# Two layers of cross attention and FFN on one core: the second cross attention unrolled to a slot for each step of a tile

## The reference

```
x += linear_attention(LN(x), ctx)      # 16 heads, gate, Wo                   "stage 0"
x += moe_ffn(LN(x))                    # top 2 of 8 experts + shared expert   "stage 1"
x += norm_delta(softmax_attention(LN(x), ctx, mask))                         # "stage 2"
x += ffn(LN(x) in float16)             # 256 -> 1024 -> 256, exact gelu       "stage 3"

softmax_attention: q = LN(x) Wq + bq; k = ctx Wk + bk; v = ctx Wv + bv   (16 heads of 16)
                   out = softmax(q k / 4, masked) v Wo + bo
norm_delta:        d = rs * out; (d - mean d) / sqrt(var d + 1e-5) * gamma + beta
```

## Time and profile before

| what | value |
|---|---|
| median of 3 runs | 499.48 us (495.07 to 500.86) |
| profiled execution | 501.04 us, span 499.2 us |
| busy, share of the span | PE 424.8 us (85%), DVE 326.5 (65%), POOL 229.5 (46%), ACT 229.2 (46%) |
| mean granted clock of TensorE | 0.896 |
| instructions | 10421 |

### The profile page before, as it was taken

How to read it: one execution, slowest core, us unless ns; L and a number is a source line. 1 busy time by engine, 2 the same in 40 slices (tenths; PEclk the granted TensorE clock), 3 DMA queues, 4 the chain that set the end, 5 groups by cost and what they waited for, 6 DMA issues and landing times. The chain is left out here.

```text
span 499.2 us, 10421 instructions
## 1 busy us (share of the span) xinstructions
PE 424.8 (85%) x3336; PEld 380.8 (76%) x3336; DVE 326.5 (65%) x904; ACT 229.2 (46%) x527; POOL 229.5 (46%) x377
## 2 busy tenths in 40 slices
PE   2999999999879678999985658786988699699995
PEld 1777888888668568999984657675877589699995
DVE  4488778777665855665548565787587747766542
ACT  4476675664332113776765253323242334354450
POOL 4355554885636502123545513777677644721200
PEclk9899998998988979999999697879577958799999
DMA  8622111224102432578653101111101000001011
GB/s 269 188 63 63 46 57 52 84 73 156 44 21 86 169 117 64 178 226 248 194 160 105 44 1 43 33 33 33 33 22 44 21 1 2 1 22 41 25 43 42
DMA packets 31731, 39.30 MB, mean 79 GB/s; under 512 B 4289, under 2 KB 29122, under 8 KB 31682
## 3 DMA queue, kind: packets, MB, share of 16 engines
q1 hardware_dynamic: 28610, 30.29, 19.8%
q0 software_dynamic: 3072, 8.39, 4.9%
HBM read 25.03 MB, written 13.63 MB: 77 GB/s over the span
## 5 line engine op out<-in xcount | busy, mean ns | idle before, releaser
L998 ACT ACTIVATE arena_f<-PS,cols 128x256 f16<-128x256 f32 x64 | 26.6, 471 | 32.4 <-PE PS L2019 30.2
L337 PE MATMUL PS<-wfh,arena_r 128*128 x120 | 36.0, 300 | 3.6 <-DVE arena_f L1445 1.9
L361 POOL TENSOR_TENSOR ve<-mv,eps 128x1 f32<-128x1 f32 x32 | 6.1, 189 | 66.5 <-DVE mv L355 66.4
L337 PE MATMUL PS<-w0h,arena_r 128*128 128x256 f32 (+1 forms) x96 | 36.6, 381 | 0.0
L378 PE MATMUL PS<-ident,arena_f 128*128 128x128 f32 x64 | 15.9, 337 | 23.8 <-DVE arena_f L370 8.5
L720 POOL DMA_INDIRECT raw<-ys_rows,posy x32 | 31.6, 989 | 9.7 <-issue 7.8
L2019 PE MATMUL PS<-arena_r,w1h 128*128 128x256 f32 x128 | 33.4, 298 | 2.0 <-ACT arena_r L1008 1.0
L468 POOL TENSOR_TENSOR w1l<-raw,w1h 128x384 fp32r<-128x384 f32 x16 | 15.0, 935 | 42.4 <-ACT w1h L455 42.4
L338 PE MATMUL PS<-wfl,arena_r 128*128 x120 | 33.9, 283 | 0.0
L339 PE MATMUL PS<-wfh,arena_r 128*128 x120 | 33.6, 280 | 0.0
L2019 PE MATMUL PS<-arena_r,w1l 128*128 128x256 f32 x128 | 32.9, 294 | 0.0
(11 more groups left out here) (278 smaller groups left out, 1524.5 us busy)
## 6 DMA issues: line engine op xcount, KB each, us to landing
arena_f<-xs_rows SPq DMA_DIRECT2D x40, 128.0 KB, 2.3
ys_rows<-raw SPq DMA_DIRECT2D x20, 256.0 KB, 2.5
raw<-in_w_ffn SPq DMA_DIRECT2D x16, 241.0 KB, 2.6
raw<-in_w_l SPq DMA_DIRECT2D x16, 192.0 KB, 3.0
ctx_raw<-in_ctxT SPq DMA_DIRECT2D x16, 128.0 KB
out<-arena_f SPq DMA_DIRECT2D x8, 256.0 KB, 2.1
x<-in_x SPq DMA_DIRECT2D x1, 1792.0 KB, 10.6
raw<-in_w_l SPq DMA_DIRECT2D x2, 512.0 KB, 5.7
```

Of the source, the lines that this page charges most:

```text
L337: nc.tensor.matmul(out_ap, lh, rh, start=first, stop=False)
L998: nc.scalar.activation(md16[:, r, n, :], PS[:, M_H + n // 2, (n % 2) * D:(n % 2 + 1) * D], ACT.Gelu, bias=cols[:, 2 * KC + n:2 * KC + n + ...
```

## The change

It has six parts:

1. The shared expert's outputs use four PSUM banks (`H_O`), so the output of tile t waits for the sum of tile t-3 (earlier: t-1); DVE's order is new, `block_table` stands after the sums of four tiles, and `result_places` in the first expert block.
2. `keys_values(p)` is cut into `keys(p)` and `values(p)`. Those of pairs 0 and 1 are made inside the block loop, and keys of pair 2 before the last down product. Ctx pairs are loaded and split earlier.
3. Gathers have a ring of six tiles; the first nine are issued before the slots.
4. The layer norm before attention and the delta's norm are ACT instructions with scale rstd and bias -mean*rstd. POOL makes both for one x tile and one delta tile, eight tiles apart, in one chain of width two (`joint_rstd`).
5. The bias bo is added on PE, by two matmuls of one row by 256 columns; ACT scales by rs (`delta`); gamma moves from POOL to DVE; POOL adds beta to x early (`add_beta`) and the delta late (`add_delta`).
6. `slot2` has one order for even and odd slots, scores have two banks of their own each (`X_S = (6, 1)`), and the steps of a tile lie more slots apart: 20 slots in place of 19 on DVE, 22 on POOL.

Cut to its core:

```diff
-H_G, H_U, H_O = (3, 6), (5, 1), (4, 2)
+H_G, H_U, H_O = (3, 6), (5, 1), (4, 2, 0, 7)
+LOAD_CTX_AT, CTX_AT, KEYS_AT = (4, 12, 14, 19), (6, 8, 16, 20), (12, 16)
+JOIN = 8
+RING = 6
...
@@ DVE, shared expert @@
+            gate_factor(4)
+            hidden(4)
             for t in range(2):
                 add_shared(t)
-            gate_factor(4)
-            add_shared(2)
-            hidden(4)
-            add_shared(3)
             hidden_lo(4)
+            for t in range(2, 4):
+                add_shared(t)
+            gate_factor(5)
+            hidden(5)
             block_table()
-            result_places()
...
@@ PE, blocks @@
+                if j in KEYS_AT:
+                    keys(KEYS_AT.index(j))
+                if j - 2 in KEYS_AT:
+                    values(KEYS_AT.index(j - 2))
                 if j == BPAIRS + 1:
-                    pe.wait_ge(w_lo, 2 * TILES)
-                    keys_values(0)
+                    keys(2)
...
@@ POOL @@
+            def joint_rstd(n):
+                kinds = slice(0 if n < TILES else 1, 2 if n >= JOIN else 1)
...
+                if n < TILES:
+                    pool.wait_ge(S2["x_moments"], 2 * n + 2)
+                if n >= JOIN:
+                    pool.wait_ge(S2["d_moments"], 2 * (n - JOIN) + 2)
+                nc.gpsimd.tensor_tensor(vej[:, at, kinds], mvj[:, at, kinds, 1], eps[:, 0:wide],
+                                        ALU.add).then_inc(S2["shifted"], 1)
...
+                nc.gpsimd.tensor_tensor(rj[:, at, kinds], vej[:, at, kinds], mhalf[:, 0:wide],
+                                        ALU.pow).then_inc(S2["shifted"], 1)
...
+                for k in range(kinds.start, kinds.stop):
+                    nc.gpsimd.tensor_scalar(sj[:, at, k:k + 1], mvj[:, at, k, 0:1], rj[:, at, k:k + 1], -1.0,
+                                            ALU.mult, ALU.mult).then_inc(S2["shifted"], 1)
...
+            def add_beta(t):
+                pool.wait_ge(xn_ready, LN_BASE[2] + t + 1)
+                nc.gpsimd.tensor_tensor(x[:, t, :], x[:, t, :], rows[:, 3, :], ALU.add).then_inc(S2["beta"], 1)
+            def add_delta(t):
+                pool.wait_ge(S2["beta"], t + 1)
+                pool.wait_ge(S2["scaled"], t + 1)
+                nc.gpsimd.tensor_tensor(x[:, t, :], x[:, t, :], dn[:, t % 2, :], ALU.add).then_inc(x_done[2], 1)
...
             def slot2(s):
+                if s.at + 3 < TILES + JOIN:
+                    joint_rstd(s.at + 3)
...
+                if tile := s.tile(-6):
+                    add_delta(tile[0])
+                if tile := s.tile(9):
                     gather(tile[0])
+                if tile := s.tile(-1):
+                    add_beta(tile[0])
...
@@ ACT @@
+            def norm_x(t):
+                act.wait_ge(S2["shifted"], shift_count(t))
...
+                nc.scalar.activation(xn[:, t % 2, :], x[:, t, :], ACT.Identity, bias=sj[:, t, 0:1],
+                                     scale=rj[:, t, 0:1]).then_inc(xn_ready, 1)
...
             def slot2(s):
+                if tile := s.tile(2):
+                    normed_hi(tile[0])
+                if tile := s.tile(-3):
+                    attended_hi2(tile[0])
+                if tile := s.tile(3):
+                    norm_x(tile[0])
+                if tile := s.tile(0):
+                    probabilities(tile[0])
+                if s.ring == 1 and s.tile(1):
+                    queries((s.at + 1) // 2)
+                if tile := s.tile(-5):
+                    delta_normed(tile[0])
+                if tile := s.tile(-3):
+                    delta(tile[0])
...
@@ PE @@
             def slot2(s):
+                if tile := s.tile(0):
+                    scores(tile[0])
+                if s.ring == 1 and s.tile(1):
+                    pair_queries((s.at + 1) // 2)
+                if tile := s.tile(-1):
+                    weighted_values(tile[0])
+                if s.is_at(TILES + 1):
+                    attended_T2(TILES - 1)
+                if tile := s.tile(-3):
+                    output(tile[0])
+                if (tile := s.tile(-2)) and tile[0] < TILES - 1:
+                    attended_T2(tile[0])
+                if tile := s.tile(3):
+                    normed_T(tile[0])
...
+                if s.is_at(TILES):
+                    pe.wait_ge(S2["clipped"], 2 * TILES)
+                    ffn_hidden(0, 0, EARLY[:4])
+                if s.is_at(TILES + 1):
+                    ffn_hidden(0, 0, EARLY[4:])
```

More of the change, by code:

```diff
@@ L986, in _ @@
+            keys(3)
+            ctx_pair_hi(5)
+            keys(4)
+            norm_x(0)
+            ctx_pair_hi(6)
             keys(5)
+            normed_hi(0)
+            norm_x(1)
             ctx_pair_hi(7)
-            for p in range(6, CPAIRS):
-                keys(p)
-            act.wait_ge(setup_v, 6)
+            keys(6)
+            normed_hi(1)
+            norm_x(2)
+            keys(7)
+            queries(0)
             def ffn_gelu(g, r, features):
@@ L1450, in block_h_lo, with values, heads @@
                                         ALU.subtract).then_inc(E["h_lo"], 1)
+            def values(p):
+                dve.wait_ge(S2["v_psum"], p + 1)
+                dve.wait_ge(S2["zeroed"], 3 * p + 3)
+                def heads(ap, b, h, r):
+                    return ap[SEQ * b:SEQ * (b + 1)].rearrange("p (r g h e) -> p r g h e", r=r, g=PAIRS, h=2)[:, :, :, h, :]
+                for b in range(2):
+                    for h in range(2):
+                        last = nc.vector.tensor_tensor(
+                            vb[p][SEQ * h:SEQ * (h + 1), :, b, :, HD * h:HD * (h + 1)],
+                            heads(PS[:, VALUES_BANK[p], :], b, h, 2),
+                            heads(rows[:, 0, :], b, h, 1).to_broadcast([SEQ, 2, PAIRS, HD]), ALU.add)
+                last.then_inc(S2["vb_ready"], 1)
             for j in range(2):
@@ L1505, in _ @@
             values(2)
             ctx_pair_lo(4)
[L1507 removed]
             values(3)
             ctx_pair_lo(5)
[L1510 removed]
+            entering(0)
             values(4)
             ctx_pair_lo(6)
[L1513 to L1514 removed]
+            entering(1)
+            values(5)
+            normed_lo(0)
+            ctx_pair_lo(7)
             entering(2)
[L1516 to L1517 removed]
@@ L1546, in _ @@
+            normed_lo(1)
+            entering(3)
+            values(7)
             cx = PS[:, X_C, 0:PAIRS * PVC].rearrange("p (g n) -> p g n", g=PAIRS)
@@ L2081, in slot2 @@
-                if s.ring == 0:
-                    if s.tile(0) and not s.is_at(0):
-                        pair_queries(s.at)
-                    if s.tile(-1):
-                        weighted_values(*s.tile(-1))
-                if s.ring == 1 and s.tile(0):
-                    scores(*s.tile(0), s.pair)
-                if s.tile(-2):
-                    output(*s.tile(-2))
-                if tile := s.tile(2):
-                    if before := s.tile(-2):
-                        after(pe, S2["cnT_lo"], before[0])
-                    transpose_x(pe, 2, *tile, X_T)
```

646 lines of the change are left out of this document (344 added, 302 removed).

## The result

Changed kernel: 482.05 us, median of 4 runs (479.88 to 484.76), beside 500.17 us of the kernel before (4 runs, 495.07 to 503.09). Ratio 0.967, 95% interval 0.958 to 0.977. It is faster, by 18 us where the prediction said 38. The profiled execution took 482.49 us (span 480.4, granted clock 0.925); the one of before 501.04.

A forecast was written before the change was run, and what follows sets the result against it. PE was taken to bound expert blocks and FFN, a chain of four engines with PE's falling clock the cross attention. First scores -12, steps -20, end -6 make -38: 501 to 463, said as 462 (454 to 470; 443 to 481 eight in ten).

The forecast's parts named there:

- Shared sums: Shared expert stage: four banks remove PE's waits and slow clock, so the blocks start 8 us earlier (4 to 9).
- Keys in the blocks: Expert blocks: PE's matmuls of two pairs cost 5.8 us, ACT's burst 1, later keys save 1.5: +5.3 us.
- Start: Last block output to first scores: POOL's queue, then ACT, takes 27.9 us instead of 36.8: -9.
- A slot for each step: Cross attention, first to last scores: steps of 5.7, then 6.5 us, plus 8 for the clock, 101 in all: -20.
- the chain through gamma: Late cross attention steps: POOL's delta add waits for DVE's gamma, delaying the next statistics; 6.5 us a step.
- The end: Last scores to steady FFN: 13.5 us instead of 18.49, plus 1 us from the FFN's start: -6 (-9 to -2).
- I take 13.5: Last scores to steady FFN: PE's remaining work 12 us, the last tile's chain 10 plus handoffs; 13.5 us taken.
- a longer queue of POOL and ACT: Cross attention: slower steps or a falling clock, 7.3 to 7.6 us a step, total 474 to 482; chance 0.24.
- The other rivals: Cross attention: no clock drop, 445 us, chance 0.20; steps staying at 8, 487, 0.07; lower clock throughout, 510, 0.04.
- the two drops: Cross attention: two falls of PE's clock, each about 1.3 steps long at 3 us a step, 8 us allowed.
- four fifths: Cross attention: share of steps at the lower clock from which the change would be slower; that rival's chance 0.04.
- The price of nothing: Cross attention: gamma on DVE charged no delay to POOL; the skill's port lock would cost some 4 us, sum 466.
- the bursts to keep the clock falling: Cross attention: short matmul bursts between waits keep lowering PE's clock, sum about 478; chance 0.24, shared with a longer queue.

The follow-up runs named there:

- e10: The kernel before with its shared sums in four banks and DVE's order left alone: 495.60 us, ratio 0.989.
- e13: Changed kernel with half of PE's products for keys and values of pairs 0 and 1 left out: blocks 76.74 us.
- e4: Changed kernel with the keys' evacuation of pairs 0 and 1 ahead of the weight split in ACT's slot: 478.57 us, ratio 0.961.
- e6: Changed kernel with POOL's memsets, gathers and statistics interleaved anew and ACT's contexts of pairs 6 and 7 ahead of norms: 488.89 us, ratio 0.972.
- e11: Changed kernel with the add of delta at the end of POOL's slot: 481.44 us, ratio 0.955.
- e3: Changed kernel with ACT's last attended values around the first four gelus and the second group's halves before the last delta norm: 474.96 us, ratio 0.954.
- e12: Changed kernel with the moves of e3, e4, e5, e6 and e11 together: 463.39 us, ratio 0.923.
- e15: e12 run again unaltered, in another call: 459.90 us, ratio 0.921.
- e8: Changed kernel with the norms of x and of delta on DVE again, slots kept: 499.55 us, ratio 1.002.
- e5: Changed kernel with gathers six tiles ahead in place of nine, one in each slot: 493.29 us, ratio 0.988.

## Why the prediction was wrong, step by step

1. **Shared sums: right in kind, the size in part by luck.** -8 said, -9.6 in the profiles. The banks alone are 5.7 us by e10's ratio; the rest lies within what the shared stage varies by, about 9 us with the same code. The waits are counts: an output of tile t waits until t-3 sums are done, that is for tile t-4 (before: t-1 sums, tile t-2), where the description of the change and the prediction name tile t-3.
2. **Keys in the blocks: wrong in its mechanism.** The step priced PE's matmuls as "5.8 us there in full" and ACT's burst at 1 (0 to 3). Halving the matmuls changed nothing beyond the spread (e13); moving ACT's burst gave 3.8 us back (e4). The 7 us that stay after e4 were not taken apart. I had asked whether ACT has room (45 of 66 us) and not what stands ahead of the keys in its queue and who waits for them.
3. **Start: the size was right for another order.** 27.9 us said, 31.7 measured, 27.7 in e6. The sum let the memsets end about when the store landed, 4.4 us after the last block output; they ended at 6.4. It counted what POOL has to do up to the third statistics and let each item start when POOL was free; ACT and DVE lost time because the statistics of tile 0 stood behind work they did not need.
4. **A slot for each step: right in size, slightly better, partly by luck.** 5.25 us a step from scores 2 to 7 (5.7 said), 6.4 from 8 to 15 (6.5 said); 95.8 us in all against 101. Two errors cancel: the lump of gathers, 8.1 us for the first step, was not seen, and the chain through gamma cost about 7 us once (95.8 us against 89.0 in e11), from slot 6 on, where a gather stands in it, not in every late step: from slot 7 on POOL has no gather left. From scores 9 to 15 a step takes 6.0 us, and 5.9 with the chain undone (e11), so the chain does not set these steps; what does was not tested.
5. **The end: the failed step, 13.9 of the 19 us.** "I take 13.5" summed the chain of the last tile and PE's work of 12 us. ACT's order cost 6.8 us (e3). With that mended PE is busy 15.5 of 19.1 us at the upper clock (e12): its work was 3.5 us more than I counted. A tile now leaves one slot later, so that four outputs and not three are left after the last scores, each with 0.43 us of bias rows, for which step 4 had charged 0.23. The fourth output and these rows are about 2.4 of the 3.5, an estimate from their rows (0.7 us for an output's product and 4 x 0.43). So ACT's order is half of the miss and PE's work a quarter; the last quarter is waits whose causes were not taken apart.

Of the rivals, "a longer queue of POOL and ACT" came nearest: 474 to 482 by a slower step. The time is right, the place is not, the steps were fast. The other rivals did not occur. Two sums of the rivals do not come out, though the forecast does not rest on them: 7.3 to 7.6 us a step are 110 to 114 us, or 118 to 122 with the two drops, not 112 to 118; and (8.05 + 1.2 - 6.3) of 3.2 is nine tenths of the steps, not four fifths.

By the Trainium skill (SBUF — State Buffer, "Who interferes with whom") each gamma on DVE should have held POOL up. The price of nothing was right, but not for the reason given, that such work shows no delay. The timelines of POOL and DVE in the kernel before:

```profile
310.86 0.34 POOL L760 TENSOR_TENSOR ve<-mv,eps 128x1 f32<-128x1 f32 x1 [3.01 <-DVE mv L1536]
311.27 0.82 POOL L763 TENSOR_TENSOR rstd<-ve,mhalf 128x1 f32<-128x1 f32 x1
313.60 0.19 POOL L361 TENSOR_TENSOR ve<-mv,eps 128x1 f32<-128x1 f32 x1 [1.51 <-DVE mv L355]
313.87 0.55 POOL L364 TENSOR_TENSOR rstd<-ve,mhalf 128x1 f32<-128x1 f32 x1
...
318.49 0.73 POOL L755 TENSOR_TENSOR x<-x,arena_f 128x256 f32<-128x256 f32 x1
318.69 0.81 DVE L1467 SCALAR_TENSOR_TENSOR x<-raw,mix,x 128x256 f32<-128x256 f32 x1
...
327.20 0.45 DVE L1467 SCALAR_TENSOR_TENSOR x<-raw,mix,x 128x256 f32<-128x256 f32 x1
```

L1467 and L1471 are DVE's two adds of a combine, with both large operands in SBUF. In nine of 16 tiles they overlap POOL's add L760, and there it takes 0.34 to 0.37 us and the power L763 behind it 0.82; in the other seven 0.19 and 0.55 to 0.56 (in two of these L1467 begins during the power, which stays at 0.56). The other way round, L1467 takes 0.77 to 0.88 us in the five tiles where it starts during POOL's add L755, and 0.45 to 0.51 elsewhere. So in this trace the two engines delay each other, as the Trainium skill has it there; averages such as those in the earlier trace rows hide it. In the changed kernel gamma seldom meets POOL, which mostly stands waiting for it: of nine gammas in the stage one overlaps a POOL instruction, a shift that took 0.47 us and not 0.26. At the end, where they meet again, both get longer (gamma takes 0.36 us alone, L723 0.19):

```profile
410.67 0.49 DVE L1676 TENSOR_TENSOR arena_f<-arena_f,rows 128x256 f32<-128x256 f32 x1 [0.38 <-ACT arena_f L1081]
...
410.84 0.37 POOL L723 TENSOR_TENSOR vej<-mvj,eps 128x1 f32<-128x1 f32 x1
```

By the Trainium skill (TensorE: Matmul & The Clock Gate, "HAM oscillation — how this bites in real kernels") I had expected the bursts to keep the clock falling; it rose from 0.75 to 0.88 in this stage and to 0.96 in e12, with the same bursts and shorter waits between them. The kernel that the Trainium skill describes there waits 3 to 5 us for a DMA between its bursts, while I had counted on waits of at most 1.7 us here, so it was no ground to expect this rival. The changed kernel's two low stretches in the stage, 292.2 to 302.4 us and 339.9 to 353.6, begin within PE's waits of 6.35 and 2.32 us; in e12 PE waits at most 1.3 us at a time from 299 us to the last scores, and the clock stays at its upper level.

## What to carry to other kernels

When work moves between engines with fixed programs, price it by its place in the queue, not by the engine's share of busy time: for every instruction that waits, write down what stands behind it and who waits for that, at the first and the last tiles above all, where a deeper pipeline adds slots that nothing fills. Order is cheap to mend: five reorderings without one instruction less gave 24 us, more than the change itself on the same chip (13 us). Mend the queues together: two of the five gained nothing alone, and for one of them (e6) the trace shows the next stage taking the gain.

## What was not expected of the hardware

The same code took different times up to the blocks: they start at 179.3 us in e15 and at 190.0 in e12, one kernel on two chips, and at 183.8 and 191.0 in e8 and e5 on one chip, where the code up to there is the same too. In some executions ACT and DVE stand idle there with nothing in the profile that holds them ("remote" or "issue"). Waits of ACT in e5, then in e15:

```profile
ACT w0h L894 <- remote: 5.8, 1, 5.8
ACT arena_f L887 <- remote: 5.1, 1, 5.1
...
ACT w0h L896 <- issue: 4.2, 2, 3.2
ACT arena_f L889 <- remote: 3.0, 2, 2.3
```

The unaltered kernel's first profile has none of that there; the kernel before has 2.2 us of "remote" on ACT and 2.4 on DVE. But this idle time does not explain the length by itself: e15 has it too and is the shortest of all. What makes the difference stays open. It makes total times of single executions poor evidence for an edit of a few us behind that point, and the length of the stage in question the better one. In e5 the ratio alone would have said that the edit costs 1 to 2%; its own stage did not change.
